# One pool of seven PSUM banks in a head attention loop, denominators inverted one stage earlier, and an addend moved to the causal stage

## The reference, cut to what matters

```python
xn = layernorm(x)                                  # x: 4 x 1024 x 256
# causal self attention on xn, one head of width 256
K, V = split(xn @ W.T)
A = xn + softmax(causal(xn K^T)) V
# feed forward layer on xn, with its own attention of 16 heads of width 16
sa = softmax(rope(q) rope(k)^T / 4) v              # per head, no mask, over 1024 tokens
x1 = rmsnorm(xn + (sa @ Wo), norm1_w)
F = rmsnorm(x1 + shared_expert(x1) + routed_experts(x1), norm2_w)
out = x + A + F
```

## Time and profile before

| what | us |
|---|---|
| median of 3 runs | 1526.81 (1516.79 to 1530.07) |
| the profiled execution | 1530.5 |
| its span in the profile | 1528.8 |
| stage 2, from the first scores to the last `finish` | 147.7 to 295.7 |
| stage 3, from the first item to the last take-out | 299.1 to 1047.4 |
| stage 4, from its first matmul | from 1053.8 |

### The profile page before, as it was taken

How to read it: one execution, slowest core, us unless ns; L and a number is a source line. 1 busy time by engine, 2 the same in 40 slices (tenths; PEclk the granted TensorE clock), 3 DMA queues, 4 the chain that set the end, 5 groups by cost and what they waited for, 6 DMA issues and landing times. The chain is left out here.

```text
span 1528.8 us, 26433 instructions
## 1 busy us (share of the span) xinstructions
PE 1401.7 (92%) x9829; PEld 818.2 (54%) x9829; DVE 1148.3 (75%) x1802; ACT 860.4 (56%) x1573; POOL 361.8 (24%) x358
## 2 busy tenths in 40 slices
PE   6999699869999999999999999888899999889995
PEld 4665577623333333333333333334788888778884
DVE  3776666596899999999999999524477777646664
ACT  2454334205788888888888888763234433323331
POOL 0333912145041000000000001001133333445553
PEclk9999899955999999999999999976899999999998
DMA  5799776152342334444433432102465555355551
GB/s 196 269 329 333 262 237 146 42 95 69 63 113 60 52 45 64 63 63 64 64 61 60 64 58 57 35 32 60 129 160 148 146 162 143 85 194 170 176 177 55
DMA packets 115040, 183.47 MB, mean 120 GB/s; under 512 B 26389, under 2 KB 65705, under 8 KB 114917
## 3 DMA queue, kind: packets, MB, share of 16 engines
q1 hardware_dynamic: 90117, 124.55, 32.4%
q0 software_dynamic: 14336, 43.61, 9.6%
q10 hardware_dynamic: 10464, 13.64, 3.0%
HBM read 100.79 MB, written 81.88 MB: 119 GB/s over the span
## 5 line engine op out<-in xcount | busy, mean ns | idle before, releaser
L1686 DVE TENSOR_REDUCE i_saT<-h_sq 128x2 f32<-128x1024 f32 x512 | 621.7, 1223 | 46.4 <-PE h_sq L1563 34.9
L1652 ACT ACTIVATE h_p<-h_sk 128x512 f32<-128x512 f32 x999 | 543.4, 595 | 160.5 <-PE h_sk L1584 136.3
L1605 PE MATMUL h_po<-h_p,h_v 128*32 128x256 f32 (+1 forms) x3840 | 336.5, 424 | 6.8 <-ACT h_o L1659 4.9
L1584 PE MATMUL h_sk<-h_q,h_k 50*128 50x512 f32 x999 | 261.2, 512 | 16.4 <-ACT h_p L1652 15.8
L1563 PE MATMUL h_sq<-h_k,h_q 48*128 48x512 f32 x1024 | 224.9, 435 | 20.8 <-DVE i_saT L1686 17.0
L1584 PEld LDWEIGHTS h_sk<-h_q,h_k 50*128 50x128 f32 x999 | 97.9, 189 | 250.6 <-ACT h_p L1652 240.4
L1605 PEld LDWEIGHTS h_po<-h_p,h_v 128*32 128x32 f32 x3840 | 77.0, 110 | 185.5 <-issue 92.1
L1957 PE MATMUL f_ob<-w_experts,f_h 128*128 x1032 | 134.5, 286 | 11.4 <-issue 9.0
L1957 PEld LDWEIGHTS f_ob<-w_experts,f_h 128*128 128x128 f32 x1032 | 125.9, 190 | 20.8 <-issue 20.7
L1563 PEld LDWEIGHTS h_sq<-h_k,h_q 48*128 48x128 f32 x1024 | 104.2, 200 | 43.1 <-DVE i_saT L1686 38.7
L1483 POOL COPY h_v<-h_values 128x512 f32<-128x512 f32 x14 | 8.6, 611 | 486.7 <-DMA h_values<-vh_d 486.7
(11 more groups left out here) (255 smaller groups left out, 1706.1 us busy)
## 6 DMA issues: line engine op xcount, KB each, us to landing
h_q<-q_d SPq DMA_DIRECT2D x84, 128.0 KB, 5.9
h_k<-k_d SPq DMA_DIRECT2D x84, 128.0 KB, 7.0
ot_d<-h_o ACTq DMA_DIRECT2D x32, 256.0 KB, 2.9
q_d<-t_parts SPq DMA_DIRECT2D x12, 512.0 KB, 5.0
k_d<-t_parts SPq DMA_DIRECT2D x12, 512.0 KB, 5.2
rows_d<-h_place SPq DMA_DIRECT2D x4, 1056.0 KB, 4.2
rows_d<-f_rows SPq DMA_DIRECT2D x4, 1056.0 KB, 4.6
p_xin<-in_L_attn_x SPq DMA_DIRECT2D x8, 512.0 KB, 5.0
```

Of the source, the lines that this page charges most:

```text
L1584: ins = nc.tensor.matmul(spread_banks[bank_at(f + g)], k6[r][at, p, j * P:(j + 1) * P], q6[r][at, p, c * CH:(c + 1) * CH], start=True, sto ...
L1605: ins = nc.tensor.matmul(po[h * VW:(h + 1) * VW, at], vh[n % RING][:, j, h, :], probs[u % PR][:, h, at], start=j == 0 and part == 0, stop= ...
L1652: nc.scalar.activation(probs[u % PR][:, h, :], spread_banks[bank_at(f)], ACT.Exp, scale=DH ** -0.5).then_inc(exp_done, 1)
L1686: nc.vector.tensor_reduce(halfmax[n % 2][:, m, :], sq[slot % 2][:, :, :], AX.X, ALU.max)\
```

## The change

Three parts. (a) In stage 3 scores, items and turned maxima take their banks from one pool of seven, by a table with a period of seven pairs. `Banks.give` remembers who held each bank; `emptied` makes PE wait for the pairs and for the items that did. Step 15 keeps five banks for pairs and two for chunk 0. (b) The sums of batches 1 and 2 are loaded at step 14, inverted by DVE in step 15, and stored to `rt_d` before stage 4; xn of chunk 1 is loaded there too; SP starts stage 4 with `load_values(2)`. (c) POOL adds xn to the rows of x in stage 2, a batch in four pieces of two tiles, each loaded by a DMA of its own; `finish` waits for its piece; `whole_ya` is gone.

```diff
 # causal_attention
+        XN_TILES = 2
+        XN_FROM = [i * XN_TILES for i in (3, 0, 2, 1)]
 ...
             @block.gpsimd
+                def add_xn(b):
+                    pool.wait_ge(rows_in[b % 2], (b // 2 + 1) * CausalInputs.LOADS * 16)
+                    for n, first in enumerate(XN_FROM):
+                        count, t0 = b * len(XN_FROM) + n, b * S + first * P
+                        at = slice(first, first + XN_TILES)
+                        if count:
+                            pool.wait_ge(xn_added, count)
+                        pool.dma_start(xn[:, :, :], xn_d[t0:t0 + XN_TILES * P, :].rearrange("(j p) d -> p j d", p=P))\
+                            .then_inc(xn_in, 16)
+                        pool.wait_ge(xn_in, (count + 1) * 16)
+                        nc.gpsimd.tensor_tensor(x[b % 2][:, at, :], x[b % 2][:, at, :], xn[:, :, :], ALU.add)\
+                            .then_inc(xn_added, 1)
+
+                add_xn(0)
                 turning.finish(pool, turning_links)
 ...
                 for n in range(HeadInputs.AHEAD):
+                    add_xn(2 * n + 1)
                     pool.wait_ge(keys_in[1], CausalInputs.LOADS * 16 * (n + 1))
-                    pool.wait_ge(rows_in[1], CausalInputs.LOADS * 16 * (n + 1))
                     heads.load(pool, n, heads_in)
+                    if n + 1 < HeadInputs.AHEAD:
+                        add_xn(2 * n + 2)
 ...
                 def finish(u):
-                    if u % QT == 0:
-                        dve.wait_ge(rows_in[b % 2], (b // 2 + 1) * CausalInputs.LOADS * 16)
+                    dve.wait_ge(xn_added, b * len(XN_FROM) + XN_FROM.index(i - i % XN_TILES) + 1)
 # head_attention
-        BANKS = 3
+        BANKS = 7
+        PAIR_BANKS = ((0, 1), (4, 0), (1, 2), (5, 6), (2, 3), (6, 0), (3, 4))
+        SLOT_BANKS = ((2, 3), (5, 6), (3, 4), (0, 1), (4, 5), (1, 2), (5, 6))
+        for h in range(LAST * UNITS * PARTS):
+            given.give(("PAIR", h), *PAIR_BANKS[h % BANKS])
+            n, m = divmod(h + ITEMS + LEAD * PER, ITEMS)
+            if m == HELD and n <= STEPS:
+                given.give(("SLOT", turn_slot(n - 1)), PAIR_BANKS[(h + 1) % BANKS][0])
+            if n < STEPS:
+                given.give(("SLOT", item_slot(n, m)), *SLOT_BANKS[h % BANKS])
+        given.give(("FIRST", 0), *OF_FIRST)
+        for h in range(LAST * UNITS * PARTS, STEPS * UNITS * PARTS):
+            given.give(("PAIR", h), *(b % OF_FIRST.start for b in (h * SIDES, h * SIDES + 1)))
 ...
             @block.sync
                         chunk.load_xn(sp, 0, routing.xn_in)
+                        for b in range(1, B - 1):
+                            chunk.load_sums(sp, b, routing.inverse[:, b, :], routing.sums_in[b])
 ...
+                routing.store_inverses(sp, sp.wait_ge, 0)
                 routing.load_inverses(sp, sp.wait_ge, 0)
                 sp.wait_ge(routing.sa_done, Routing.SA)
                 chunk.load_values(sp, 1, routing.values_in)
                 routing.load_inverses(sp, sp.wait_ge, 1)
+                for half in range(2):
+                    sp.wait_ge(*first.released(("WO", 0, half)))
+                chunk.load_xn(sp, 1, routing.xn_in)
+                for b in range(1, B - 1):
+                    routing.store_inverses(sp, sp.wait_ge, b)
+                sp.wait_ge(routing.inverses_stored, (B - 1) * 16)
 ...
+                def emptied(key):
+                    pairs, slots = given.before_it(key, "PAIR"), given.before_it(key, "SLOT")
+                    if pairs:
+                        pe.wait_ge(exp_done, max(h * SIDES + g + 1 for h, g in pairs))
+                    if slots:
+                        pe.wait_ge(sq_free, max(slot + 1 for slot, _ in slots))
                 def item(n, m):
-                    pe.wait_ge(sq_free[slot % 2], slot // 2)
+                    emptied(("SLOT", slot))
                 def score(n, w, p):
-                        pe.wait_ge(exp_done, max(emptied) + 1)
+                    emptied(key)
 ...
             @block.vector
                 routing.squares(dve, 0)
+                for b in range(1, B - 1):
+                    routing.invert(dve, b)
 # feed_forward
             @block.gpsimd
-                def whole_ya(c): ...
-                whole_ya(0)
-                    if c < LASTS:
-                        whole_ya(c + 1)
 ...
             @block.sync
                 def load_values(c):
                     inputs.load_values(sp, c, routing.values_in)
+                    if c == (B - 1) * S // CH:
+                        routing.store_inverses(sp, wait.ge, B - 1)
                     routing.load_inverses(sp, wait.ge, c)
 ...
+                load_values(2)
                 load_ya(0)
+                inputs.load_sums(sp, B - 1, routing.inverse[:, B - 1, :], routing.sums_in[B - 1])
                 load_ya(1)
-                for b in range(1, B):
-                    inputs.load_sums(sp, b, routing.inverse[:, b, :], routing.sums_in[b])
-                load_xn(1)
 ...
-                load_values(2)
 ...
-                        if f < B - 1 and c == 0:
-                            routing.invert(dve, f + 1)
+                        if f == 2 and c == 0:
+                            routing.invert(dve, B - 1)
```

More of the change, by code:

```diff
@@ L958, in released, with __init__, give, before_it @@
         return self.free_of(key), self.n[key] // len(self.buffers) + 1
+class Banks:
+    def __init__(self):
+        self.holder, self.places, self.before = {}, {}, {}
+    def give(self, key, *banks):
+        self.places[key] = banks
+        self.before[key] = [self.holder[b] for b in banks if b in self.holder]
+        for i, b in enumerate(banks):
+            self.holder[b] = (*key, i)
+    def before_it(self, key, kind):
+        return [(n, i) for was, n, i in self.before[key] if was == kind]
 class Room:
@@ L1183, in invert, with store_inverses @@
         self.nc.vector.reciprocal(self.inverse[:, b, :], self.inverse[:, b, :]).then_inc(self.inverted, 1)
+    def store_inverses(self, eng, wait, b):
+        wait(self.inverted, b + 1)
+        self.chunk.store_inverses(eng, b, self.inverse[:, b, :], self.inverses_stored)
     def load_inverses(self, eng, wait, c):
-        b = c // 2
-        if c % 2 == 0:
-            wait(self.inverted, b + 1)
-            self.chunk.store_inverses(eng, b, self.inverse[:, b, :], self.inverses_stored)
-        wait(self.inverses_stored, (b + 1) * 16)
+        wait(self.inverses_stored, (c // 2 + 1) * 16)
         self.chunk.load_inverses(eng, c, self.values_in)
@@ L1409, in head_attention @@
         mparts = sb("h_mparts", [TILES, SHIFT, P], F32R)
-        sk = [ctx.enter_context(nc.psum_tensor(f"h_sk{i}", [P, CH], F32)) for i in range(BANKS)]
-        sq = [ctx.enter_context(nc.psum_tensor(f"h_sq{i}", [P, SIDES, CH], F32)) for i in range(2)]
-        spread_banks = [s[:, :] for s in sk] + [sq[0][:, g, :] for g in range(SIDES)]
-        LAST = (STEPS - 1) * FILLS
-        bank_at = lambda f: f % BANKS if f < LAST else (f - LAST + LAST % BANKS) % len(spread_banks)
-        latest, before = {}, []
-        for f in range(STEPS * FILLS):
-            before.append(latest.get(bank_at(f)))
-            latest[bank_at(f)] = f
+        banks = ctx.enter_context(nc.psum_tensor("h_banks", [P, BANKS, CH], F32))
         po = ctx.enter_context(nc.psum_tensor("h_po", [P, CH], F32))
@@ L1442, in head_attention @@
         first_free = sems("h_first_free", SIDES)
-        first = Fills([sq[1][:, g:g + 1, :] for g in range(SIDES)], first_made, first_free,
+        OF_FIRST = range(BANKS - SIDES, BANKS)
+        first = Fills([banks[:, b:b + 1, :] for b in OF_FIRST], first_made, first_free,
                       [("WO", 0, 0), ("WO", 0, 1), ("XT", 0, 0), ("XT", 0, 1), ("GATE", 0), ("RANK", 0)])
@@ L1455, in turn_slot, with both_banks, bank_of @@
             return (n + 1) * ITEMS + n + (HELD if n + 1 < STEPS else 0)
+        LAST = STEPS - 1
+        PAIR_BANKS = ((0, 1), (4, 0), (1, 2), (5, 6), (2, 3), (6, 0), (3, 4))
+        SLOT_BANKS = ((2, 3), (5, 6), (3, 4), (0, 1), (4, 5), (1, 2), (5, 6))
+        given = Banks()
+        for slot in range(turn_slot(0) + LEAD * PER - HELD + 1):
+            given.give(("SLOT", slot), *(SLOT_BANKS[3 + slot % 2] if slot != turn_slot(0) else (6,)))
+        for h in range(LAST * UNITS * PARTS):
[8 more added lines that the diff above has]
+            given.give(("PAIR", h), *(b % OF_FIRST.start for b in (h * SIDES, h * SIDES + 1)))
+        def both_banks(key):
+            low, high = given.places[key]
+            return banks[:, low:high + 1, :]
+        def bank_of(key, i=0):
+            return banks[:, given.places[key][i], :]
         ROOT_AT, TURN_AT, GATES_AT, EXP_AT, COUNT_AT = 8, 10, 11, 14, 15
@@ L1825, in _ @@
             def _(pool):
-                def whole_ya(c):
-                    pool.wait_ge(routing.xn_in, (c + 1) * 16)
-                    pool.wait_ge(ya_in[c % 2], (c // 2 + 1) * 16)
```

(8 more changed lines are left out.)

47 lines of the change are left out of this document (23 added, 24 removed).

## The result

The changed kernel takes 1536.02 us (median of 20 runs, 1523.64 to 1546.26), the kernel before 1522.91 beside it (20 runs, 1513.44 to 1534.76). The ratio is 1.0098, with 1.0074 to 1.0121 as its 95% interval: it is about 1% slower, 13 us by the medians and 15 by the ratio, where 7.4 us less were forecast. The profiled execution took 1544.88, its span is 1543.1, which is 14.3 more than the 1528.8 of before.

The account below looks back on a forecast made before the run. It took PE as the bound in stages 2 and 3, and in stage 4 except for a 7.55 us stop in chunk 0. Terms 20 - 16 - 11.4 = -7.4 gave 1519.4 us, range 1503 to 1540.

Parts of the forecast that it names:

- Part (c): Stage 2: POOL's additions of xn cost +20 us, bounds +14 to +45.
- The first stall: Stage 2: DVE's first `finish` of batch 1 waits for POOL's piece until 227.9, 20.0 us late.
- They meet. I take +20: End of stage 2: POOL ends near 316, PE at 315, so only the first stall's cost was counted, about +20.
- The second rival: POOL ends stage 2 late: at 7 us a piece the sum is +18, time 1544; chance 0.15.
- Part (b): Chunk 0 of stage 4: early inverses remove the 7.55 us stop and half clock behind it, -11.4 us, bounds 6 and 13.
- `i_tot` of chunk 2 is there some 10 us after the start: Start of stage 4: `load_values(2)` needs no store, so `head(2)` doesn't wait and the 7.55 us stop goes.
- The 0 for taking `whole_ya` from POOL: Stage 4: removing it frees no PE time, since PE isn't waiting for it: 0.
- Part (a): Stage 3: the bank pool saves 1.14 us a step in 14 steps, -16 us, bounds -30 to +15.
- The three terms: Stage 3, saved per step: normal pairs 0.25 us, take-outs 0.56, turning 0.33; sum 1.14.
- The first rival: Stage 3: the pool gives nothing because PE's floor is 1.23 a pair; sum +8.6, time 1535; chance 0.16.
- Added waits at 0: Stage 3: one more wait on each pair and item costs 0, being already met when PE comes to it.
- The fourth rival: Stage 3: the clock comes back sooner, about 17 us at stake, time 1504 or the other way; chance 0.09.

Follow-up runs that it names:

- The order experiment: Changed kernel with POOL adding batch 1 ahead of `turning.finish` and batch 2 ahead of the stores, still one buffer: 1538.28 us, ratio 1.0105 to before.
- Part (b) alone: The kernel before with only the early inverses added, SP's loads of stage 4 in the order of before: 1519.55 us, ratio 0.9975.
- (c) alone: The kernel before with only POOL's additions of xn in stage 2 and without `whole_ya`: 1547.03 us, ratio 1.0183.
- (a) and (b) alone: The kernel before with the bank pool and the early inverses, its causal stage, `whole_ya` and SP's stage 4 order kept: 1505.42 us, ratio 0.9894.
- the late inversion: DVE inverts the sums of batch 3 in chunk 1 instead of chunk 0; as the only edit to the changed kernel: 1525.71 us, ratio 1.0021 to before.
- the last kernel: All three parts, two xn buffers, batch 3 inverted in chunk 1, and batch 2 added ahead of the twelve head loads: 1496.69 us, ratio 0.9819 to before.

## Why the prediction was wrong

- **Part (c), forecast +20, measured +27.9 alone, +27.2 in the profile.** The first stall was sized right: 227.9 against 227.07. The step that failed is the one behind it: "They meet. I take +20". I allowed 8 us of contention for POOL's tail and nothing for PE's side. They did meet, but both later: POOL's end was 320.2 against 316, PE's side 319.9 against 315. The landings behind `heads.load` were 11.01 and 6.28 against 2.8, 11.7 us more, which made batch 2 late once more, and the end of the stage came 2.5 us later behind the last `finish`. The order experiment shows what the sum didn't say: with the first stall taken away stage 2 ends no earlier, since POOL's chain is as long (321.8 with its last copy, where 320.2 stood). The second rival (POOL ends stage 2 late) had the right place. Its price, 7 us a piece, was wrong: the usual piece takes 5.0, where I had put 5.2.
- **Part (b), forecast -11.4, measured -3.8 alone, -2.4 in the profile.** This is the largest miss. The step that failed is "`i_tot` of chunk 2 is there some 10 us after the start": I took the 18.5 us of rows 11 for the store's, and let the load land at once. Part (b) alone kept 4.63 us of stop, since DVE gets that load 22.2 us behind its issue. In the changed kernel the load is early enough, and the sums of batch 3, which the prediction never followed, are late instead. The 0 for taking `whole_ya` from POOL failed in its reason too: PE's time in chunk 0 is the same with (c) alone (47.08 against 47.73), but that is luck, with one stop gone and another in its place. The size of the stop and of the half clock behind it was right: taking the last one away gave 9.0 us in chunk 0, 11.4 against before (47.73 to 36.36).
- **Part (a), forecast -16, measured -10.2 in the fourteen steps, -9.3 alone.** The three terms were the right ones and each was too large: normal pairs 0.1 for 0.25 a step, take-outs 0.47 for 0.56, the turning 0.21 for 0.33. The normal pairs did not come to 1.23: behind a take-out of the changed kernel the pair follows the half `mix` after 0.57 nearly each time and takes 0.34 + 0.33 to the next half `mix`, 1.24 in all. PE's floor that is not: the five pairs behind the turning shown are 1.226 apart (626.31 to 632.44). What sets the 1.24 stays open. The first rival is right for the normal pairs, wrong for the rest. Added waits at 0: nothing against it. What the Trainium skill ("Perfetto Trace Analysis", Identifying Dependency Chains) says, that separate semaphore instructions may stand ahead of an instruction with several waits, shows no price here: with one more wait on each pair and item the pairs are 1.239 apart instead of 1.243. Up to 0.01 a pair could hide in the 1.239, where 1.23 was expected.
- **The clock.** The fourth rival named a stake of 17 us in the rise. Step 1 takes 43 to 57 us in twelve profiles, at a mean granted clock of 0.54 before, 0.58 in the changed kernel and 0.67 with (a) and (b) alone; 49.6 (0.67) and 43.1 (0.80) belong to two kernels with the same stages 2 and 3. Much of the 23 us range of single runs may be that; what moves the rise stays open, and no reading above rests on it.
- **POOL's DMAs and DVE.** The Trainium skill ("SBUF — State Buffer", the warning on GpSimd's DMAs) was given as a reason for long pieces. The warning is on DVE's two-port mode, a condition that the prediction left out, and no row here shows that mode. No stall shows: fifteen of sixteen pieces were issued in 0.72 to 0.74 us with DVE at work, and the long ones are long in their landing, the two longest behind the loads of `heads.load`.

The sum of the terms as measured, 27.2 - 10.2 - 2.4, is +14.6 where +20 - 16 - 11.4 was written. Each term lay within its bounds except that of (b), whose lower bound was 6. All three erred towards a gain. 1536 lies between 1503 and 1540, but that is no merit of the sum: the change costs time where a gain was forecast.

## What to carry to other kernels

When work is handed to an engine that "has air", write its whole queue from end to end with the landing of each transfer in it; where loads and uses share one buffer the landings stand in a row, and a second buffer (with a better order) gave what an order alone did not (here 1.0021 to 0.9872, against 1.0098 to 1.0105). When a load is moved to the front of a queue, go through everything that is now behind it and the next instruction that needs it: the stop of 16 us here came from a load of 512 KB that six others had been put in front of. A stop of 6 us came from a load of 64 KB that nobody had followed. And what is taken away moves things too: without one addition of POOL its next stores went out 5.6 us earlier, beside those loads. Measure a change of several parts part by part: the same three parts, with a second buffer, another order of POOL and the late inversion, are 1.8% faster than before, and as they stood 1% slower.

## What the hardware did that was not expected

- In the changed kernel POOL mostly waits 2.3 to 2.9 us for a load of 256 KB that it has issued, and 11.0 us (9.5 and 7.0 in two other kernels) for one issued behind twelve loads of 128 KB on its own queue. Those loads aren't the only reason: in the last kernel two pieces in front of them were waited for 5.48 and 3.85 us.
- At the start of stage 4 small loads land as late as large ones. The broadcast inverses were used 22.1 and 21.7 us behind their issue in two kernels, whether `ya_d` of chunk 1 and the sums were ahead of them or behind. The list of DMA issues of the changed kernel between 1050 and 1110 us (KB each, us to landing) has the same for others. What holds them up was not tried; the four index stores of POOL, issued from 1066.27 on, are a suspect (see part (c) alone):

```profile
h_place<-ya_d SPq DMA_DIRECT2D x1, 512.0 KB, 22.6
f_rows<-ya_d SPq DMA_DIRECT2D x1, 512.0 KB, 18.8
...
h_place<-ot_d SPq DMA_DIRECT2D x1, 64.0 KB, 22.3
```

- Large operations of POOL slow DVE's split of the values. In the timeline of before the first two take 10.14 us together, beside `turning.finish`; in the changed kernel, where POOL waits for its first landing, 2.36. PE's wait of 7.7 us behind them is gone, and batch 0 ends 7.8 us earlier (206.33 and 198.54); with the stage 2 of before it ended between 203.5 and 209.4 in six profiles. In the changed kernel a later split, at 184.44 and again beside `turning.finish`, takes 4.11 where 1.21 is usual. This gain of part (c) was not in the forecast; the stall behind it ate it. Before, and after:

```profile
159.68 10.14 DVE L835 TENSOR_TENSOR a_v<-c_va,a_v 128x1024 fp32r<-128x1024 f32 x2 [2.73 <-ACT a_v L776]
```

```profile
159.24 2.36 DVE L856 TENSOR_TENSOR a_v<-c_va,a_v 128x1024 fp32r<-128x1024 f32 x2 [1.14 <-ACT a_v L798]
```
